# A four-layer graph network on one core: 1,361 semaphore updates of TensorE sent by a drain behind the last matmul

## What is computed

```python
def norm(x): return relu(layernorm(x))
h = norm(x)                                  # layer 0: GIN with batch norm
z = (1 + eps) * h + segment_sum(h[src], dst)
x = x + relu(bn(relu(bn(z @ W1 + b1)) @ W2 + b2 + h))   # 256 -> 512 -> 256
h = bn(norm(x))                              # layer 1: gated, weighted edges both ways
a_in = segment_sum((h @ Win + bin)[src] * iw, dst)
a_out = segment_sum((h @ Wout + bout)[dst] * ow, src)
x = x + gru(concat(a_in, a_out) @ Wx2i, h @ Wh2h)
h = norm(x)                                  # layer 2: GIN again, 256 -> 256 -> 256
x = x + relu(bn(relu(bn((h + segment_sum(h[src], dst)) @ W1)) @ W2))
h = norm(x)                                  # layer 3: an MLP on every edge
m = relu(concat(h[dst], h[src] - h[dst]) @ W1 + b1) @ W2 + b2   # 512 hidden
x = x + segment_sum(m, dst) / count(dst)
```

## Time and profile before

| what | value |
|---|---|
| time, median of 3 runs | 3428.49 us (3427.81 to 3428.86) |
| the profiled execution: its span | 4205.1 us |
| PE busy | 2930.9 us, 70% |
| PEld busy | 1849.8 us, 44% |
| DVE busy | 2117.9 us, 50% |
| ACT busy | 1141.1 us, 27% |
| POOL busy | 2373.5 us, 56% |

### The profile page before, as it was taken

The page is one execution under the profiler, slowest core; times in us unless marked ns, Lnnn a source line. Parts: engine busy times, 40 slices in busy tenths (PEclk is TensorE's granted clock), DMA queues, the critical chain, the costliest instruction groups (busy, mean ns, idle before and its releaser), DMA issues. The chain is left out here.

```text
span 4205.1 us, 55362 instructions
## 1 busy us (share of the span) xinstructions
PE 2930.9 (70%) x11580; PEld 1849.8 (44%) x11581; DVE 2117.9 (50%) x6459; ACT 1141.1 (27%) x3023; POOL 2373.5 (56%) x2458
## 2 busy tenths in 40 slices
PE   3677776555542846677588887755554899988989
PEld 1233333333321434444333332433333548888878
DVE  6566664333320455444456655533333576667664
ACT  1466661000000330000000000300000356666662
POOL 3544445666667046666666666666666226666662
PEclk6788887667665867888799999976676999999999
DMA  3000002333320043333366666433333136666664
GB/s 123 2 1 1 1 1 74 90 89 90 90 56 2 20 139 88 101 106 105 109 176 180 177 176 178 138 89 89 87 91 86 34 124 186 187 188 185 189 187 143
DMA packets 184321, 438.94 MB, mean 104 GB/s; under 512 B 53924, under 2 KB 78623, under 8 KB 184233
## 3 DMA queue, kind: packets, MB, share of 16 engines
q0 software_dynamic: 135568, 372.32, 31.3%
q1 hardware_dynamic: 48665, 65.55, 4.7%
HBM read 403.39 MB, written 34.24 MB: 104 GB/s over the span
## 5 line engine op out<-in xcount | busy, mean ns | idle before, releaser
L834 POOL DMA_INDIRECT acc<-table,stg_idx x1170 | 1128.5, 965 | 767.8 <-issue 349.1
L2116 PE MATMUL psum<-acc,oh 128*128 x2600 | 871.4, 489 | 637.7 <-issue 456.5
L2116 PEld LDWEIGHTS psum<-acc,oh 128*128 128x128 f32 x2600 | 598.2, 244 | 912.3 <-issue 821.2
L1497 DVE TENSOR_TENSOR acc<-acc,psum 128x257 f32 (+1 forms) x660 | 276.0, 418 | 962.7 <-remote 565.4
L1032 ACT CAST stg_idx<-rec 128x2 int32 (+1 forms) x784 | 148.4, 193 | 2113.0 <-remote 841.2
L945 POOL DMA_INDIRECT TT<-qtable,stg_row x440 | 424.1, 964 | 282.4 <-PE psum L2428 150.9
L860 POOL DMA_INDIRECT H<-gtable,stg_idx x391 | 379.1, 970 | 199.5 <-issue 116.5
L2205 PE MATMUL psum<-H 125*128 125x440 bf16 x1600 | 375.5, 399 | 154.2 <-issue 48.2
L2137 PE MATMUL psum<-H,oh 128*128 x880 | 426.2, 630 | 79.8 <-issue 31.1
L810 POOL DMA_INDIRECT recs<-acc,sst_idx x290 | 284.6, 981 | 338.1 <-ACT acc L977 255.6
L2428 PE MATMUL psum<-oh,TT 128*128 128x128 f32 x3520 | 444.3, 277 | 34.7 <-issue 26.0
(11 more groups left out here) (277 smaller groups left out, 3210.7 us busy)
## 6 DMA issues: line engine op xcount, KB each, us to landing
acc<-table,stg_idx POOLq DMA_INDIRECT x1173
TT<-loc_dram SPq DMA_DIRECT2D x22, 320.0 KB
TT<-qtable,stg_row POOLq DMA_INDIRECT x440
Wm<-loc_dram SPq DMA_DIRECT2D x22, 320.0 KB
H<-gtable,stg_idx POOLq DMA_INDIRECT x391
gtable<-H SPq DMA_DIRECT2D x24, 256.0 KB
qtable<-H SPq DMA_DIRECT2D x24, 256.0 KB, 2.2
table<-H SPq DMA_DIRECT2D x8, 640.0 KB
```

Of the source, the lines that this page charges most:

```text
L834: pool.indirect_dma_start(out=dst[:, c, 0:D], out_offset=None, in_=src, in_offset=bass.IndirectOffsetOnAxis(ap=stg_idx[:, c:c + 1], axis=0 ...
L1497: V.tensor_tensor(at, at, sum_bank(j)[:, 0:w], ALU.add).then_inc(added, 1)
L2116: last = mm(sum_bank(j)[:, 0:w], oh[:, 2 * j + k, :], rows_flat[:, ds(start[j] + k * S, w)], start=(k == 0), stop=(k == 1))
```

## The change

In three places the update no longer hangs on the last matmul of a group. Behind that matmul stands a `drain`, an instruction of TensorE's own stream that is done when all matmuls before it are, and the drain carries the update. The places are the placement (`used`, 400 updates), the units of passes one to four (`summed`, 880) and, in `done`, the stages z0, up0, down0 and back0 (`filled`, 81). Updates of all other stages stay on their matmul or transpose. No matmul, wait, table or order is changed. The stream of each engine reads the same as before but for the drains.

```diff
@@ -81,6 +81,7 @@
 WREST = GROUPS - WITS * RING_W
 GST = 5
 PRE_AT = FOLD_AT + 5
+BESIDE_SCATTERS = ("z0", "up0", "down0", "back0")
 assert 0 < WREST < RING_W <= RING_G and UNITS % GST == 0 and PRE_AT + UNITS < ITERS
 assert NT + UNITS < ITERS and GITS * RING_G == GROUPS and ITERS * SP_IT == GROUPS + NB - 1 and HALF_U <= P
 assert FOLD_AT + 6 < ITERS
@@ -1989,7 +1990,10 @@
                 return ps[b]
 
             def done(ins, st, k):
-                ins.then_inc(filled[bank(st, k)], 1)
+                if st in BESIDE_SCATTERS:
+                    nc.tensor.drain().then_inc(filled[bank(st, k)], 1)
+                else:
+                    ins.then_inc(filled[bank(st, k)], 1)
 
             def counts(o, turn):
 
@@ -2115,7 +2119,7 @@
                     for k in range(2):
                         last = mm(sum_bank(j)[:, 0:w], oh[:, 2 * j + k, :], rows_flat[:, ds(start[j] + k * S, w)],
                                   start=(k == 0), stop=(k == 1))
-                    last.then_inc(summed, 1)
+                    nc.tensor.drain().then_inc(summed, 1)
 
                 return unit
 
@@ -2203,7 +2207,7 @@
                     pe.wait_ge(weighed, i * COLS + k0 + 1)
                     for k, ring in enumerate((src_ring, code_ring, top_ring, low_ring)):
                         last = mm(ps[k][:, 0:CHUNKS], ring[:, c, :], hi_ring[:, c, :], start=False, stop=False)
-                    last.then_inc(used, 1)
+                    nc.tensor.drain().then_inc(used, 1)
             for k in range(PARTS):
                 last = mm(ps[k][:, 0:CHUNKS], zero16[:, 0:P], zero16, start=False, stop=True)
             last.then_inc(placed, 1)
```

## The result

The changed kernel takes 4320.69 us (median of 4 runs, 4307.1 to 4324.49), the kernel before 3428.15 us (4 runs, 3426.13 to 3428.86): ratio 1.26, 95% interval 1.2584 to 1.2615, +892 us. The forecast was 4,430 in a range of 3,480 to 4,850.

A forecast was written before the change was run, and what follows sets the result against it. POOL's gathers were taken to pace the passes, 463 us each. Added time for passes one and four, two, three, placement and dense layer, 264 + 289 + 237 + 165 + 45 = 1,000, on 3,428 gives 4,430 us; range 3,480 to 4,850.

The forecast's parts named there:

- Direction and mechanism: Whole kernel: slower, 0.82, because what ran under the matmuls waits behind each drain and units start cold; +1,000 us.
- The steps: TensorE's sequencer between two cold units: 0.4 us bare in the passes, 0.3 us in the placement.
- The drain's own lag: Each drained update: comes 0.05 us later than from the matmul, costing nothing beside a ring of five banks.
- The loading: Passes, tables for the next five units: stands bare behind a drain, taken as 2.3 us between bounds 1.4 and 2.8.
- Passes: Passes one to four: lengthen to 595, 752, 700 and 595 us, or +132, +289, +237 and +132.
- The clock: TensorE in passes one, two and four: stretched matmuls bring three quarters of the time at 1.2 GHz, against three fifths.
- the sign named: Profile of passes one, two and four: granted clock below 0.70 if the forecast is right.
- POOL's pace: Passes in a timed run before the change: a gather each 1.185 us, 463 us a pass.
- The holds: TensorE's updates while POOL issues: wait behind profiler records, 16 x 0.70 = 11.2 us a group; all absent from timed runs.
- Faster: Four passes and late scatters: timed runs have held updates and a drain's update passes them; about 3,300 us, chance 0.14.
- TensorE keeps 2.4 GHz: TensorE throughout: clock stays high, passes one and four +0, two +65, three +205; 3,908 us, chance 0.27.
- Short steps: Behind each drain: sequencer needs 0.15 us and table loads 0.55; 3,683 us, down to 3,480, chance 0.13.

The follow-up runs named there:

- The run with bare drains: The changed kernel with all 1,361 drains in place but each update left on its matmul: 4878.07 us, ratio 1.1595 to the kernel before.
- more records without work: The kernel before, no drain, two more one-row, one-column matmul calls in each unit of passes one and four: 4245.32 us, ratio 1.007.

## Why the forecast held, point by point

**Direction and mechanism: right.** The drain serialises the units, the sequencer's steps and the table loading stand bare behind it, and where TensorE then needs more than POOL, POOL waits for ScalarE's casts. The run with bare drains shows that it is the standing, not the update. Drains in pass three alone, in the placement alone and tables loaded ahead each move a part of it in the forecast's way.

**The steps.** A bare step between units: 0.4 forecast, 0.42 measured; 0.3 and 0.32 in the placement. A unit's cycle: 1.53 and 2.48 forecast, 1.55 and 2.50 measured. A column: 1.20 forecast, 1.22 measured. The drain's own lag: 0.05 from the end of the program, 0.02 measured. **The loading** was taken too low: 0.4 + 2.3 forecast between turns, 3.65 measured in passes one and four (two loads of 1.24, and 1.2 of steps; some 3.0 in two and three), so a turn at the low clock is 15.4 us, not 14.7.

**Passes.** Forecast 595, 752, 700, 595, in all 2,642; measured 586, 654, 719, 678, in all 2,637. The sum fits by luck, because two misses cancel. Pass two was given 157 us for its products and is 68 us longer than pass one. Pass four was given three quarters of low clock and had it throughout (0.50), pass one had less of it (0.71). These two passes run the same units but for one column in 257, 678 and 586 us: 92 us lie between a clock that is low all the time and one that is low for about three fifths of it. That is an estimate of the clock's price, read from one trace. **The clock** itself moved less than the forecast had it: the sign named was a granted clock below 0.70 in passes one, two and four, and it is 0.71, 0.74 and 0.50, against 0.70, 0.78 and 0.70 in the trace of before. In pass one the stretched matmuls did not lower it.

**POOL's pace: the term that was mis-sized.** I took a gather in a timed run at 1.185 us, 463 us a pass. In the free trace POOL still issues one each 1.26 us wherever it does not wait, and at that pace a pass can't be under 391 x 1.26 = 493 us. The four passes were thus 1,972 us at least and lose at most 665 us, not 790. That is 125 us, more than the 109 between 4,430 and 4,321; placement and dense layer give the rest back. The rest of the balance is an estimate, as no free trace of the kernel before exists, and takes its passes at POOL's pace: the stretches of the free trace that the change leaves alone are 4,317 - 497 - 2,637 - 33 = 1,150 us (33 for what of the dense layer stands behind the late scatters), which leaves 3,428 - 1,150 - 1,972 = 306 us for placement and dense remainder before; at 0.74 us a column the placement was 297. So the placement lost some 200 us where 165 were forecast, and the dense layer some 20 where 45 were, which the +25 us of the run with drains in that layer alone doesn't contradict, though it was held.

**The holds: the step that was wrong in its reason.** That holds were absent from the 3,428 us was right, and the base of the sum stood on it. "I take it that a timed run, which nobody profiles, writes no such records" is not borne out: timed runs beside the experiments took 4,213 us, with holds, and the changed kernel's free trace has its records and no hold. "16 x 0.70 = 11.2" describes one stretch, but half of TensorE's work and more records without work show that the number of TensorE's records does not set what a held pass costs, and the held trace of the changed kernel has holds without a step of 0.70 us. What the recording may still have to do with it: the same changed kernel left 52,466 semaphore updates in its free trace and 24,459 in its held one. The Trainium skill's page NOTIFIC — the notification-queue block, section 7.1, says that the block pushes back on its producers rather than lose a record inside. Held executions would fit such a path, but no run here tells it from another cause.

**The rivals.** "Faster" fails at its mechanism: a drain's update does not pass a hold: held, the changed kernel takes 4,918 us beside 4,258, and in the run with one drain a turn 71 of 130 drains end late. "TensorE keeps 2.4 GHz" fails on 0.71, 0.74 and 0.50. "Short steps" fails on 0.42 and 3.65. The chances given to them, 0.14, 0.27 and 0.13, came from not trusting rows of a held trace; the rows held.

**Open.** Whether a chip, its surroundings or the way of recording makes an execution held was not settled: the held ones came on four chips, and the free pair is known only from the result. No part of the change was measured alone in a free execution: the +892 us are split by the free trace of the changed kernel and the balance above, not by runs. How much of the 50 to 61 us that passes one, two and four keep with tables ahead comes from late drains and how much from the low clock is open too. No version beat the kernel before by more than 0.3%.

## What to carry to other kernels

A drain on TensorE costs almost nothing itself in a free execution (0.02 us behind the last matmul), but it bares everything that used to run under the matmuls: here 0.42 us a unit, 3.65 us where register loads follow, and in pass four a lower clock besides (0.50 against 0.70). If one must stand in a stream, issue loads and register work ahead of it. Before you subtract two traces, compare a stretch that the change doesn't touch: here the last layer, 621 and 704 us for the same code.

## What the runs showed of the hardware

The same kernel takes 3,426 to 3,429 or 4,204 to 4,259 us (the changed one 4,307 to 4,324 or 4,916 to 4,920). The traces of the longer ones show updates of TensorE that stay away while POOL issues indirect DMAs and for the most part arrive when POOL pauses for some 4 us; in the second trace of the kernel before the longest wait named "remote" is 17.4 us for an index cast and 74.8 us for ScalarE's evictions beside the late scatters. Halving TensorE's work in pass one does not change it (573 us). A drain ends 20 to 23 ns behind the last matmul in the free trace; in held ones some end 10 us and more behind it, and the longest, behind five units, stands for 41 us.
